# First layer of a four-layer kernel: second score tile over all 128 rows, first batch split by VectorE, its rows asked for by SyncE

## What is computed

```python
a = _layer_norm(audio_kv, ln_gamma, ln_beta)          # audio_kv: the context
Q = (hidden_states @ Wq.T).reshape(B, Tt, 16, 16).transpose(0, 2, 1, 3)
K = (a @ Wk.T)...;  V = (a @ Wv.T)...                 # same shape
scores = jnp.where(mask, einsum('bhtd,bhsd->bhts', Q, K) * scale, -inf)
out = einsum('bhts,bhsd->bhtd', softmax(scores), V)
return hidden_states + tanh(gate) * (out @ Wo.T)
```

## Time and profile before

| | us |
|---|---|
| runs: median of 3 (lowest, highest) | 1280.21 (1278.9, 1288.83) |
| the profiled execution | 1286.75 |
| its span, first to last instruction | 1284.9 |
| PE busy in the span | 1218.2 (95%) |
| DVE, ACT, POOL busy | 792.6, 538.6, 216.4 |
| mean granted TensorE clock | 0.983 |

### The profile page before, as it was taken

How to read it: one execution, slowest core, us unless ns; L and a number is a source line. 1 busy time by engine, 2 the same in 40 slices (tenths; PEclk the granted TensorE clock), 3 DMA queues, 4 the chain that set the end, 5 groups by cost and what they waited for, 6 DMA issues and landing times.

```text
span 1284.9 us, 17676 instructions
## 1 busy us (share of the span) xinstructions
PE 1218.2 (95%) x5936; PEld 836.4 (65%) x5936; DVE 792.6 (62%) x2354; ACT 538.6 (42%) x1233; POOL 216.4 (17%) x429
## 2 busy tenths in 40 slices
PE   6999988999897879999998999999999999999998
PEld 4554553646463444444443788888888888888887
DVE  5545348868684356878865666666666666666520
ACT  2354534444353335455554443434333434343332
POOL 3231034334243121120101101000000000000000
PEclk8899999999998799999999999999999999999999
DMA  7557322020205444525335703030303030500000
GB/s 232 135 127 227 105 107 90 26 82 25 75 33 145 168 134 150 158 81 161 134 121 200 262 1 132 1 132 1 132 1 132 1 132 1 197 1 1 1 9 25
DMA packets 95033, 124.42 MB, mean 97 GB/s; under 512 B 7264, under 2 KB 72960, under 8 KB 92704
## 3 DMA queue, kind: packets, MB, share of 16 engines
q1 hardware_dynamic: 94320, 123.00, 29.8%
q10 hardware_dynamic: 624, 0.30, 0.1%
HBM read 79.33 MB, written 43.65 MB: 96 GB/s over the span
## 4 chain that ended last, share of the span: by engine, by line
PE 82%; DMA 5%; DVE 4%; ACT 3%; issue 2%; POOL 2%; SPq 2%; ACTq 0%; POOLq 0%; DVEq 0%
PE J L2468 9%; PE J L2488 9%; PE TT L2476 9%; PE TT L2452 4%; PE S L2442 4%; PE OO L2442 4%; PE OO L1092 4%; PE OO L1095 4%; PE TT L657 2%; PE J L324 2%; PE J L1361 2%; PE OO L2709 2%; PE J L1095 2%; PE J L333 2%; PE S L324 2%
## 5 line engine op out<-in xcount | busy, mean ns | idle before, releaser
L2546 ACT ACTIVATE PT<-TT 128x512 f32<-128x512 f32 x128 | 76.4, 597 | 279.9 <-PE TT L2452 279.9
L2581 POOL COPY On<-probs 128x8 f32<-128x8 f32 x128 | 29.2, 228 | 470.0 <-DVE probs L2616 440.7
L2627 DVE TENSOR_SCALAR QK<-J,cols 128x256 f32<-128x256 f32 x126 | 61.0, 484 | 68.5 <-PE J L2468 68.5
L2616 DVE TENSOR_SCALAR probs<-probs,inv 128x257 f32<-128x257 f32 x256 | 79.1, 352 | 4.5
L2452 PE MATMUL TT<-ident,probs 128*128 128x128 f32 x512 | 76.9, 273 | 2.6 <-DVE probs L2616 2.6
L2452 PEld LDWEIGHTS TT<-ident,probs 128*128 128x128 f32 x512 | 63.8, 141 | 16.4 <-DVE probs L2616 3.8
L1092 PE MATMUL OO<-weights_a,ctxT 128*128 128x512 f32 x136 | 67.6, 620 | 6.0 <-SPq L308 3.1
L2622 DVE COPY km<-TT 128x256 f32<-128x256 f32 x128 | 54.2, 424 | 30.6 <-PE TT L2476 30.3
L1095 PE MATMUL OO<-ctxT,weights_a 128*128 128x512 f32 x136 | 66.4, 611 | 6.0 <-SPq L308 3.5
L2335 DVE TENSOR_TENSOR_SCAN early<-km,early 128x256 f32<-128x256 f32 x64 | 64.3, 1045 | 10.9 <-ACT early L2106 10.1
L1639 DVE CUSTOM_DVE_ANT_0 mask_b<-S,early 128x256 f32<-128x256 f32 x128 | 48.7, 418 | 28.1 <-PE S L1331 28.1
(11 more groups left out here) (414 smaller groups left out, 2651.4 us busy)
## 6 DMA issues: line engine op xcount, KB each, us to landing
wide_keys<-weights_a SPq DMA_DIRECT2D x64, 256.0 KB, 2.1
wide_values<-weights_a SPq DMA_DIRECT2D x56, 256.0 KB, 2.0
weights_a<-wide_keys SPq DMA_DIRECT2D x16, 512.0 KB, 7.3
weights_a<-wide_values SPq DMA_DIRECT2D x16, 512.0 KB, 8.3
early<-wide_keys SPq DMA_DIRECT2D x16, 512.0 KB, 8.1
early<-wide_values SPq DMA_DIRECT2D x16, 512.0 KB, 9.4
query_parts<-weights_a SPq DMA_DIRECT2D x32, 192.0 KB, 2.7
weights_a<-in_L_xattn_wv SPq DMA_DIRECT2D x2, 2048.0 KB, 9.9
```

The source lines that it names most:

```text
L2546: act.activation(PT[:, n % 2, :], T0[:, :], ACT.Copy).then_inc(pt3_ready, 1)
L2616: ins = dve.tensor_scalar(P_[n % 2][:, qt, :], P_[n % 2][:, qt, :], inv[:, qt, n % 32:n % 32 + 1], None, ALU.mult)
```

## The change

1. `transposed_scores` reads the second tiles over all 128 rows. GpSimd sets the second half of all four query buffers to zero first (`zeros0_ready`), so that the added rows contribute nothing.
2. Keys and queries of batch 0 are both split by VectorE, right behind its memsets and ahead of the second batch's statistics and the mask. Before, GpSimd split the keys, and VectorE the queries later.
3. SyncE asks for batch 0's key rows as soon as the key parts are kept, then keeps the query parts and asks for their rows, then asks for all rows of m = 1, and only then keeps batch 1. Ahead of m = 3 it waits for the first maxima to land.
4. Unit 0 moves ahead of the second batch's flip on TensorE (and its copy on ScalarE); the other seven units move towards the end of the steps before 0.
5. Statistics, roots and centring of batches 2 and 3 move by two or three, two or three, and one step.

```diff
-        FIRST_AT = [-13, -11, -9, -7, -6, -5, -3]
+        FIRST_AT = [-13, -11, -7, -6, -4, -3, -2]
...
             keep_keys0(sp, 0)
+            sp.wait_ge(ones0_ready, 1)
+            spread_keys0(sp, 0)
             keep_queries0(sp, 0)
-            sp.wait_ge(ones0_ready, 1)
-            spread0(sp, 0)
+            sp.wait_ge(zeros0_ready, len(q_rows0))
+            spread_queries0(sp, 0)
+            spread0(sp, 1)
             keep_keys0(sp, 1)
-            spread0(sp, 1)
             keep_queries0(sp, 1)
             spread0(sp, 2)
+            sp.wait_ge(max0_landed, 16)
             spread0(sp, 3)
...
                         for s in range(2):
-                            top = (P, REST0 + PARTS)[s]
                             mm = pe.matmul(RING0[at % 3][:, hh * S:(hh + 1) * S],
-                                           k_rows0[n % 4][0:top, s, h, kt * P:(kt + 1) * P],
-                                           q_rows0[n % 4][0:top, s, h, :], start=(s == 0), stop=(s == 1))
+                                           k_rows0[n % 4][:, s, h, kt * P:(kt + 1) * P],
+                                           q_rows0[n % 4][:, s, h, :], start=(s == 0), stop=(s == 1))
...
                 root(1)
+                for rows_ in q_rows0:
+                    pool.memset(rows_[:, 1, :, :], 0.0).then_inc(zeros0_ready, 1)
                 root(2)
-                for b in (0, 1):
-                    split_keys(b)
+                split_keys(1)
                 for at in range(-LEAD0, LAST0):
                     n, i = at // CHUNKS0, at % CHUNKS0
                     following = prepared(n)
-                    if n in (-1, 0) and i == 0:
-                        root(n + 4)
                     if i == 2 and 0 <= n + 1 < STEPS0:
                         split_maxima(n + 1)
+                    if n in (-1, 0) and i == 3:
+                        root(n + 4)
...
                     if n in (-1, 0):
-                        if i == 0:
+                        if i == 2:
                             statistics(n + 3)
-                        if i == 5:
+                        if i == 6:
                             centre_a(n + 3)
```

More of the change, by code:

```diff
@@ L495, in build @@
         pad0_cleared, pad0_ready, ones0_ready = names0("pad0_cleared"), names0("pad0_ready"), names0("ones0_ready")
+        zeros0_ready = names0("zeros0_ready")
         def rows0(region):
@@ L712, in pe_program @@
                 pe.wait_ge(loaded["x"], 16)
[L713 to L720, removed]
                 def first_unit(u):
@@ L727, in first_unit @@
                     project_ahead(pe, (J1, O0)[u % 2], u)
+                flip_x(1, J0)
+                pe.wait_ge(loaded["ctxT"], 16)
+                pe.wait_ge(loaded["quarter"], 16)
                 first_unit(0)
+                flip_a(1, O1)
+                pe.wait_ge(keys0_ready, 1)
+                keys(1, T0)
+                pe.wait_ge(queries0_ready, 1)
+                queries(1, T1)
                 for at in range(-LEAD0, LAST0):
@@ L868, in act_program @@
                 fetch_a(1, O1)
+                copy_first(act, (J1, O0)[0], 0)
                 fetch_keys(1, T0)
@@ L873, in act_program @@
                 act.wait_ge(mask_ready, 4)
-                copy_first(act, (J1, O0)[0], 0)
                 for at in range(-LEAD0, LAST0):
@@ L919, in split_keys @@
                 def split_keys(b):
-                    split0(pool, "k", keys0_ready, keys0_split, b + 1, split0_step, 2 * b + 2 * max(b - 2, 0))
+                    split0(pool, "k", keys0_ready, keys0_split, b + 1, split0_step, 2 * b - 2 + 2 * max(b - 2, 0))
                 def split_queries(b):
-                    split0(pool, "q", queries0_ready, queries0_split, b + 1, split0_step, 4 * b - 2)
+                    split0(pool, "q", queries0_ready, queries0_split, b + 1, split0_step, 4 * b - 4)
                 def split_maxima(m):
@@ L977, in split_queries @@
                 def split_queries(b):
-                    split0(dve, "q", queries0_ready, queries0_split, b + 1, split0_first, 2 * b)
+                    split0(dve, "q", queries0_ready, queries0_split, b + 1, split0_first, 2 * b + 2)
                 def take_maxima(m, f):
@@ L1022, in dve_program @@
                 ins.then_inc(ones0_ready, 1)
+                split0(dve, "k", keys0_ready, keys0_split, 1, split0_first, 0)
+                split_queries(0)
                 dve.wait_ge(loaded["ctx"], 16)
                 statistics(1)
+                dve.wait_ge(pad0_ready, 1)
+                fetch_values(0, O0)
+                centre_a(1)
                 dve.wait_ge(loaded["mask0"], 16 * 2)
@@ L1030, in dve_program @@
                 dve.tensor_scalar(mask0T, mask0T, 2.0, None, ALU.mult).then_inc(mask_ready, 1)
-                centre_a(1)
                 dve.wait_ge(mask_ready, 4)
-                split_queries(0)
-                dve.wait_ge(pad0_ready, 1)
-                fetch_values(0, O0)
                 split_queries(1)
```

## The result

The change takes 1273.24 us (median; 1267.93 to 1278.61), the kernel before 1284.86 (1278.9 to 1290.34) in the runs beside it: a ratio of 0.9904, 95% interval 0.9887 to 0.9922, so about 12 us less. The forecast was 19.3 us less (1261 us against 1280.21, which was the median of the three runs known then). The direction was right; the size was not, and the time lies above the range. The base has a part in that: counted from 1284.86, 19.3 us less would have been 1265.6, so of some 12 us between forecast and result 4.6 are the base and 7.7 the smaller gain. The profiled execution of the change took 1278.61 us, the longest of its 16 runs; it has a span of 1276.8 us, 8.1 less than that of before. Its first layer ends 10.3 us sooner, at 160.15 instead of 170.43 us; the rest of the program came out 2.2 us longer.

The account below looks back on a forecast made before the run. TensorE was taken to set the pace in the first layer's groups; start and groups summed to -21.3 us, +2.0 for a clock fall made -19.3, so 1280.2 became 1261 us, own range 1256 to 1266, 8 in 10 within 1253 to 1270.

Parts of the forecast that it names:

- Costed at nothing: the zeroing on GpSimd: Four memsets at the start, 7.1 us, while GpSimd waits for the second statistics: no cost, up to 7 if uncovered.
- the start: First layer before the first scores: they would start at 49.0 us, +0.8, bounds -1.2 and +3.
- The height: Score matmuls of each step: at full height four take 0.43 us, 0.41 less per step, 26.2 us over 64 steps.
- The groups: The first layer's stretches of eight steps for one value of n, numbered 0 to 7; eight steps are worth 3.3 us.
- Groups 0 and 1: First two eight-step stretches: -5.4 us (to 13.6, part from a higher clock) and -3.0 us.
- Groups 2 and 6: Third and seventh eight-step stretches: -3.3 us, and -2.6 us with 0.7 given back for GpSimd's split of the last maxima.
- Group 3: Fourth eight-step stretch: -2.6 us, with 0.7 of 3.3 taken back for a fill's wait for rows.
- Groups 4 and 5: Fifth and sixth eight-step stretches, ending in waits for maxima's DMA: -0.6 and -1.5 us; a clock fall gives back +2.0.
- it has to let the same bulk pass: Group 4: the small maxima DMA, issued earlier, still waits behind 2 MB of weights and stores; about 0.1 us shorter.
- Transfers set the pace everywhere: Rival, chance 0.13: maxima take 6.4 us in groups 2, 3 and 6 too; gain 10.9 us, 1269 us.
- Slower: Rival, chance 0.02: the new start order keeps TensorE at its lower clock, +15 us; about 1285 us with height bringing 10.
- Full gain: Rival, chance 0.15: small DMAs keep pace, no new pause, the clock holds; gain 26.3 us, 1254 us.

Follow-up runs that it names:

- half-price memsets: The change with its four zeroed regions written by GpSimd at the same place as 128x1024 f32 words instead of 128x2048 bf16 elements: 1268.61 us, ratio 0.9888.
- the paced run: The change with GpSimd's zeroing behind the first centring, plus stores and weights held until certain maxima have landed: 1260.14 us, ratio 0.9806.

## Why the prediction was wrong, and where it was right

**The step that failed** is "Costed at nothing: the zeroing on GpSimd", and with it the start, "+0.8, bounds -1.2 and +3"; it measured +9.8. The step looked at what queues behind the memsets on GpSimd (the next root), priced the four at 7.1 us, right to the tenth, and named 7 us as the uncovered cost. It didn't ask which other engine the memsets would hold up. Of the 9.0 us between forecast and start, 4.9 are the hold: the runs with the zeroing behind the centring and with the half-price memsets both start at 53.1. There was a cover, but of about 3 us for a hold of 6.7, and it came from TensorE's wait for unit 0's weights, not from GpSimd's idle time. Against the run with the zeroing behind the centring the fills start 3.6 us late; the rest, 1.2 us, goes between fills and scores, where TensorE waits 2.8 us for VectorE instead of 1.0. The sign of it stood in the earlier trace rows: VectorE's first operation of a split took 1.51 us beside GpSimd and 0.68 alone. I used that row for the split and not for the zeroing (there GpSimd ran a subtraction, not a memset, so it was a hint and no proof). The Trainium skill, "SBUF — State Buffer", Who interferes with whom, says that VectorE in its two-port modes, which a tensor_scalar can enter, and GpSimd lock each other out, the first to issue winning for the whole instruction. The trace agrees on who blocks (5.50 before 5.59; 7.09 us instead of 0.41); on how long it differs, below.

**The rest of the start**, 4.1 us, belongs to the new order. I put the last ask for the first query rows 0.7 us before the present 26.46. SyncE's rows of the change with the zeroing behind the centring:

```profile
21.51 1.91 SPq L561 DMA_DIRECT2D weights_a<-key_parts  x3
23.47 0.58 SPq L563 DMA_DIRECT2D weights_a<-key_parts  x1
24.09 0.95 SPq L542 DMA_DIRECT2D query_parts<-weights_a  x2
27.55 1.82 SPq L571 DMA_DIRECT2D km<-query_parts  x3
29.41 0.58 SPq L574 DMA_DIRECT2D km<-query_parts  x1
```

The last ask comes at 29.41, 3.0 later than before: the query parts stand behind four requests for key rows that take SyncE from 21.51 to 24.05, and their rows can be asked for only when the parts have landed. I had named this dependence and given the requests ahead of it no time. Fills start at 32.94 instead of the forecast 29.8. The order alone, with 19 rows, starts fills at 32.49 and scores at 49.95, within the bounds given. Here the clock fell behind the wait of 3.85 us; there it did not behind the one of 3.48, and the way from fills to scores took 17.46 us instead of 20.15. That makes 2.7 of the 3.1 us between the two; no score runs in that stretch, so the height has no part in it. Why the clock fell in one and not in the other stays open.

**The height** was right: 0.43 forecast for four scores, 0.44 measured; alone it brings the whole gain. In the trace of the change full-height loads of 98 to 103 ns (means by form) fit inside a spacing of 0.11 us, and 0.40 us of each step are gone with the changes of height. Of the Trainium skill's rules, the one on the drain ("TensorEngine Tiling (Array Packing)", Key Properties) fits this, if going from 128 to 19 rows is a change of mode, which no run here shows by itself; the one on weight loads ("TensorE: Matmul & The Clock Gate", Part 3) does not.

**The groups** were right: 20.1 forecast, 20.0 measured up to the layer's end. Groups 0 and 1 were forecast at 13.6 and 13.4 and took 13.64 and 13.47. Groups 2 and 6 came out 0.9 and 0.8 us longer than forecast. Group 2 holds a wait of 0.78 for GpSimd's split of the maxima, which I had put into group 6 alone; group 6 holds it as forecast (0.67), and then its last eight scores take 1.51 us up to the next start, with a wait for ScalarE, where 0.88 were expected. Group 3 came out 0.4 shorter: the wait for rows that I had taken back did not come. The layer's tail made up 1.5: its last eight matmuls ran at the full clock (1.99 us instead of 3.45).

**Groups 4 and 5** were right in mechanism and size: I leaned to "it has to let the same bulk pass", which would shorten group 4 by 0.1 us, and then took 0.6; it was 0.13. The wait was forecast as 3.2 and was 3.54. The clock fell behind it (0.57 from 120 to 124 us), group 5 took 13.89 against 14.4. Here the forecast had luck: with the zeroing behind the centring, 3.50 us of wait in the same place left it at 1.00, and group 5 took 12.63.

**The rivals.** "Transfers set the pace everywhere" gave 1269 us, nearest to the time, but by another way and by luck: transfers bound only groups 4 and 5. "Slower" named the start as the place and the low clock as the means; the start was the place, the means was a hold on VectorE that no rival had. "Full gain" at 1254 us is close to what the kernel gives when the hold, the bulk and the late first maxima are all taken out: 1257.76, 27 us below before against its 26.3.

## What to carry to other kernels

Before an instruction on GpSimd is costed at nothing, ask what VectorE runs in the same microseconds, not only what queues on GpSimd; at the start of a chain that TensorE waits for, put it behind VectorE's work, and write zeros in the widest words. A stage that gets shorter exposes what it hid: list the transfers issued within it and put small urgent ones ahead of bulk by a wait on their landing. An edit made of several parts is worth taking apart: here one part brings 1.5%, one next to nothing, and one takes back a third.

## What the runs showed of the hardware

- GpSimd's hold on VectorE can outlast the instruction. The first centring, 0.41 us of work, waited through four memsets of 1.81 us (7.09 us), through 16 of 0.52 (7.57), through four of 0.95 (3.68); with the zeroing alone, on the kernel before, it got in after two (3.60), its second instruction took 1.97, and the last two memsets took 1.94 instead of 1.81. What decides when VectorE gets in is open. VectorE's f32 memsets (0.91 us) ran beside the same GpSimd memsets unhindered. The Trainium skill, "SBUF — State Buffer", Who interferes with whom, has the lock held for the whole instruction; here it outlasted three more.
- GpSimd's memset is priced by elements, not bytes: 128x2048 bf16 1.81 us, 128x1024 f32 of the same bytes 0.95. The Trainium skill, "VectorE: DVE Perf Modes", Zero memsets can be issued as uint32 (trn2), says so of VectorE.
- A DMA of 12 KB took at most 2.3 us from issue to landing with the bulk held back, and about 8.2 us passed until TensorE could go on with 3.3 MB issued in the same 3 us.
- The length of a pause alone did not tell whether TensorE's clock fell to its lower level. It fell behind waits of 2.17 us (before), 2.84 (the paced run), 3.54 (the change), 3.51 (zeroing on VectorE) and 3.85, and stayed at 1.00 behind 2.21 (the change, ahead of group 6), 2.56, 3.48 and 3.50 (the end of group 4 with the zeroing behind the centring).
